# Retention loop: scores, sums and state products two tiles behind the transposes instead of one, with three buffers for v

## The reference

```python
x = x + retention(layernorm(x))            # B, T, C = 4, 1024, 256; 16 heads of 16
q, k, v = split(h @ w_qkv.T)               # h is the normed x
q, k = rope_xpos(q, k)                     # a rotation with a decay, per head
scores = einsum('bhtd,bhsd->bhts', q, k) * 16 ** -0.5
scores = scores * decay_mask               # causal, gamma ** (t - s) per head
y = einsum('bhts,bhsd->bhtd', scores, v)
yn = group_norm(y)                         # over a head's 16 channels and all T
out = (silu(h @ w_gated.T) * yn) @ w_proj.T
```

## Time and profile before

| | us |
|---|---|
| median of 3 runs | 1362.44 (1359.52 to 1365.13) |
| span of the profiled execution | 1357.2 |
| TensorE busy, share of the span | 1148.5, 85% |
| VectorE busy | 926.0, 68% |
| ScalarE busy | 613.3, 45% |
| GpSimd busy | 551.3, 41% |

### The profile page before, as it was taken

The page is one execution under the profiler, slowest core; times in us unless marked ns, Lnnn a source line. Parts: engine busy times, 40 slices in busy tenths (PEclk is TensorE's granted clock), DMA queues, the critical chain, the costliest instruction groups (busy, mean ns, idle before and its releaser), DMA issues. The chain is left out here.

```text
span 1357.2 us, 34954 instructions
## 1 busy us (share of the span) xinstructions
PE 1148.5 (85%) x14041; PEld 820.0 (60%) x14041; DVE 926.0 (68%) x1959; ACT 613.3 (45%) x1310; POOL 551.3 (41%) x537
## 2 busy tenths in 40 slices
PE   7999999976599999478999898898996658999970
PEld 4677777754488888235555555555554437888860
DVE  4778787757765656568678695968756376565646
ACT  2334343313255555144737455474635233555544
POOL 3333333202377776324151432415141115777750
PEclk9999999978699999698999999999999778999995
DMA  8032222108743332200000001000000095333338
GB/s 302 24 126 93 81 90 83 64 1 296 248 169 104 103 105 90 75 31 3 33 3 33 24 12 33 3 33 4 1 3 2 18 389 166 103 104 101 104 101 345
DMA packets 50683, 125.66 MB, mean 93 GB/s; under 512 B 7649, under 2 KB 26977, under 8 KB 47713
## 3 DMA queue, kind: packets, MB, share of 16 engines
q1 hardware_dynamic: 36896, 86.20, 17.7%
q0 software_dynamic: 13632, 37.24, 8.7%
HBM read 79.63 MB, written 43.78 MB: 91 GB/s over the span
## 5 line engine op out<-in xcount | busy, mean ns | idle before, releaser
L1090 POOL DMA_INDIRECT ffn_xs<-xn_rows,ffn_from_row x142 | 137.6, 969 | 123.7 <-DVE ffn_second_y_at L1472 81.0
L1098 POOL DMA_INDIRECT y_rows<-ffn_ys,ffn_to_row x142 | 140.1, 987 | 55.1 <-issue 35.4
L1253 PE MATMUL ffn_ps_h<-ffn_w_high,ffn_xst 128*128 x568 | 155.3, 396 | 0.6 <-issue 0.6
L1500 DVE TENSOR_TENSOR ffn_act_in<-ffn_silu_g,ffn_ps_h 128x256 f32<-128x256 f32 x142 | 59.9, 422 | 139.0 <-ACT ffn_silu_g L1132 139.0
L1132 ACT ACTIVATE ffn_silu_g<-ffn_ps_h 128x256 f32<-128x256 f32 x142 | 54.8, 386 | 144.3 <-PE ffn_ps_h L1253 144.3
L1273 PE MATMUL ffn_ps_o<-ffn_w,ffn_act_t 128*128 x284 | 117.2, 435 | 0.5 <-DVE ffn_act_t L1505 0.5
L1253 PEld LDWEIGHTS ffn_ps_h<-ffn_w_high,ffn_xst 128*128 128x128 f32 x568 | 97.4, 190 | 18.2 <-issue 1.1
L1833 POOL TENSOR_TENSOR rec_mixed_w<-rec_mixed_w,rec_xnt 128x512 f32<-128x512 f32 x16 | 17.2, 1091 | 207.5 <-DVE rec_mixed_w L2634 207.5
L1253 PE MATMUL ffn_ps_h<-ffn_w_low,ffn_xst 128*128 x284 | 89.8, 398 | 0.0
L644 DVE TENSOR_TENSOR ret_probs<-ret_score,ret_causal 128x2048 f32<-128x2048 f32 x32 | 73.3, 2292 | 18.7 <-PE ret_score L485 18.7
L1275 PE MATMUL ffn_ps_o<-ffn_w,ffn_act_t 128*128 x284 | 79.2, 279 | 0.0
(11 more groups left out here) (353 smaller groups left out, 2894.8 us busy)
## 6 DMA issues: line engine op xcount, KB each, us to landing
home<-y_rows SPq DMA_DIRECT2D x30, 512.0 KB, 5.0
w_split<-home SPq DMA_DIRECT2D x24, 512.0 KB, 4.1
ffn_w_high<-w_split SPq DMA_DIRECT2D x8, 1024.0 KB, 8.8
ffn_w_low<-w_split SPq DMA_DIRECT2D x8, 1024.0 KB, 10.7
ffn_w<-w_split SPq DMA_DIRECT2D x8, 1024.0 KB, 14.4
home<-in_f_w SPq DMA_DIRECT2D x12, 512.0 KB, 6.1
xn_rows<-home SPq DMA_DIRECT2D x12, 512.0 KB, 11.7
out<-x SPq DMA_DIRECT2D x8, 512.0 KB, 5.7
```

What stands on the lines that cost most here:

```text
L1090: pool.indirect_dma_start(xs[:, n % SLOTS, :], None, xn_rows[:], bass.IndirectOffsetOnAxis(ap=from_row[:, n:n + 1], axis=0)) \
L1098: pool.indirect_dma_start(y_rows[:], bass.IndirectOffsetOnAxis(ap=to_row[:, m:m + 1], axis=0), ys[:, m % SLOTS, :], None).then_inc(ys_stor ...
L1253: mm = pe.matmul(ps_h[:, u % 2, :], one_pass(xst[:, u % 2, part, k, :]), one_pass(w1[w_part][k][:, bass.ds(e, E_COLUMNS)]), start=(part + ...
L1500: dve.tensor_tensor(act_in[:, u % 2, :], silu_g[:, u % 2, :], ps_h[:, u % 2, FF:2 * FF], ALU.mult) \
```

## The change

TensorE's list for tile i becomes: transposes of x of i, scores of i-2, gate of i, the group norm's variance or the output's matmul, the projection of q and k of i, transposes of q and k of i-1, the projection of v of i, the group mean (t = 2) or the fourth output matmul (t = 7), outputs of i-2. The loop has two turns more at the end. `outputs` makes state times q for both halves, then the state product, then all sums. The state product moves to the bank of y, and a function `sums_read` makes its user wait for the y copy and for `add_state` of the tile before. `roped`, `v` and `v_heads` get three buffers. The gate is made before v, and its copy ahead of v's. VectorE does mask before rotate, and spread_q a tile later; group-norm steps move (`gn_half` of the second half to t = 2, `gated` to t = 4 and 5, the moments of the next batch to the end of t = 6). In GpSimd's list sum_state is a tile later and stands ahead of ln_root.

```diff
-        roped = sb("roped", [P, 2, 2 * C])
+        roped = sb("roped", [P, BUFFERS, 2 * C])
         rope_t1 = sb("rope_t1", [P, 2 * C])
         rope_t2 = sb("rope_t2", [P, 2 * C])
-        v = sb("v", [P, 2, C])
-        v_heads = sb("v_heads", [P, 2, NH, PAIR])
+        v = sb("v", [P, BUFFERS, C])
+        v_heads = sb("v_heads", [P, BUFFERS, NH, PAIR])
...
-        ps_state = ps_qkt[:, 0:KT * PAIR]
         ps_yp = ps("ps_yp", [P, BANK])
-        ps_y = ps_yp[:, 0:C]
+        ps_y, ps_state = ps_yp[:, 0:C], ps_yp[:, C:C + KT * PAIR]
...
                     pool.wait_ge(rope_parts, (i + 1) * 3)
-                    if i >= 2:
-
-                        pool.wait_ge(y_in_psum, i - 1)
-                    pool.tensor_tensor(roped[:, i % 2, :], rope_t1[:], rope_t2[:], ALU.add).then_inc(rope_done, 1)
+                    if i >= BUFFERS:
+
+                        pool.wait_ge(y_in_psum, i - BUFFERS + 1)
+                    pool.tensor_tensor(roped[:, i % BUFFERS, :], rope_t1[:], rope_t2[:], ALU.add).then_inc(rope_done, 1)
...
                 ln_root_first()
                 ln_root(0)
-                for i in range(TILES):
+                for i in range(TILES + 2):
                     b, t = step_of(i)
+                    if state_of(i - 3):
+                        sum_state(i - 3)
+                    if i >= TILES:
+                        continue
                     if t == TPB - 2 and b < B - 1:
                         ln_root(b + 1)
-                    if state_of(i - 2):
-                        sum_state(i - 2)
                     sum_rotation(i)
...
-                    if i >= 2:
-                        y_out(i - 2)
-                    v_out(i)
+                    gate_out(i)
                     if b > 0 and t == 4:
                         normed(b - 1, 0)
-                    gate_out(i)
-                    qk_out(i)
+                    if i >= 1:
+                        qk_out(i - 1)
+                    v_out(i)
                     if b > 0 and t == 4:
                         normed(b - 1, 1)
                     if 5 <= i < 5 + 2 * PIECES and i % 2 == 1:
                         split_high((i - 5) // 2)
+                    if i >= 2:
+                        y_out(i - 2)
+                qk_out(TILES - 1)
                 y_out(TILES - 2)
...
+                def sums_read(i):
+
+                    if i >= 1:
+                        pe.wait_ge(yt_ready, i)
+                        if states_before(i):
+                            pe.wait_ge(state_masked, states_before(i))
+
                 def outputs(i):
                     b, t = step_of(i)
                     pe.wait_ge(v_ready, (i + 1) * 3)
+                    sums_read(i)
+                    n_pairs = pairs_through(i + 2)
+                    if n_pairs:
+                        pe.wait_ge(x_added, n_pairs)
+                    n_steps = gn_read_through(i + 2)
+                    if n_steps:
+                        pe.wait_ge(gn_step, n_steps)
+                    if t >= 2:
+                        pe.wait_ge(state_ready, sums_before(i))
+                    for k in range(KT if t >= 1 else 0):
+                        for g in range(GROUPS):
+                            rows = slice(g * PAIR, (g + 1) * PAIR)
+                            pe.matmul(ps_y[rows, k * P:(k + 1) * P], state[rows, k, :], qkt[rows, i % 2, k, :],
+                                      start=(k == 0), stop=False, skip_group_check=True)
                     if t < TPB - 1:
-
-                        pe.wait_ge(qkt_ready, min(i + 2, TILES))
                         for k in range(KT):
                             for g in range(GROUPS):
                                 rows = slice(g * PAIR, (g + 1) * PAIR)
                                 own = slice(k * P + g * PAIR, k * P + (g + 1) * PAIR)
                                 mm = pe.matmul(ps_state[rows, k * PAIR:(k + 1) * PAIR],
-                                               roped[:, i % 2, C + own.start:C + own.stop], v[:, i % 2, own],
-                                               start=True, stop=True)
+                                               roped[:, i % BUFFERS, C + own.start:C + own.stop], v[:, i % BUFFERS, own],
+                                               start=(t == 0 and k == 0), stop=True, skip_group_check=True)
                         mm.then_inc(state_in_psum, 1)
-                    if i >= 1:
-                        pe.wait_ge(yt_ready, i)
-
-                        n_pairs = pairs_before(i + 2)
-                        if n_pairs:
-                            pe.wait_ge(x_added, n_pairs)
-                        n_steps = gn_read_before(i + 2)
-                        if n_steps:
-                            pe.wait_ge(gn_step, n_steps)
-                    if t >= 1:
-                        pe.wait_ge(state_masked, states_before(i))
-                    if t >= 2:
-                        pe.wait_ge(state_ready, sums_before(i))
+                    pe.wait_ge(probs_ready, i + 1)
                     for k in range(KT):
-                        for g in range(GROUPS if t >= 1 else 0):
-                            rows = slice(g * PAIR, (g + 1) * PAIR)
-                            pe.matmul(ps_y[rows, k * P:(k + 1) * P], state[rows, k, :], qkt[rows, i % 2, k, :],
-                                      start=True, stop=False)
-                        if k == 0:
-                            pe.wait_ge(probs_ready, i + 1)
                         for h in range(2):
                             for g in range(GROUPS):
                                 mm = pe.matmul(ps_y[g * PAIR:(g + 1) * PAIR, k * P:(k + 1) * P],
-                                               v_heads[:, i % 2, k * HPT + 2 * g + h, :], probs[:, g, k, h, :],
-                                               start=(h == 0 and t == 0), stop=(h == 1))
+                                               v_heads[:, i % BUFFERS, k * HPT + 2 * g + h, :], probs[:, g, k, h, :],
+                                               start=False, stop=(h == 1), skip_group_check=True)
                     mm.then_inc(y_in_psum, 1)
...
-                for i in range(TILES):
+                for i in range(TILES + 2):
                     b, t = step_of(i)
-                    transpose_x(i)
+                    if i < TILES:
+                        transpose_x(i)
+                    if i >= 2:
+                        scores(i - 2)
+                    if i == 0:
+                        project_qk(i)
+                        pe.wait_ge(early_consts_loaded, 16 * len(early_consts))
+                    if i < TILES:
+                        gate(i)
+                    if i == TPB - 1:
+                        pe.wait_ge(consts_loaded, 16 * len(consts))
+                    if 0 < b < B and t in (3, 5, 6, 7):
+                        sums_read(i - 2)
+                        if t == 3:
+                            group_variance(b - 1)
+                        else:
+                            projection(b - 1, t - 5, ps_yp)
+                    if 0 < i < TILES:
+                        project_qk(i)
+                    if 1 <= i <= TILES:
+                        transpose_qk(i - 1)
+                    if i < TILES:
+                        project_v(i)
+                    if 0 < b < B and t == 2:
+                        sums_read(i - 2)
+                        group_mean(b - 1)
+                    if 0 < b < B and t == TPB - 1:
+                        pe.wait_ge(x_added, b * PAIRS - 1)
+                        projection(b - 1, PAIRS - 1, ps_yp)
                     if i >= 2:
                         outputs(i - 2)
-                    project(i)
-                    if i == TPB - 1:
-                        pe.wait_ge(consts_loaded, 16 * len(consts))
-                    if b > 0 and t in (2, 3, 5, 6, 7):
-
-                        pe.wait_ge(yt_ready, i - 1)
-                    if b > 0 and t == 2:
-                        group_mean(b - 1)
-                    if b > 0 and t == 3:
-                        group_variance(b - 1)
-                    if b > 0 and t >= 5:
-                        projection(b - 1, t - 5, ps_yp)
-                    if i >= 1:
-                        scores(i - 1)
-                    gate(i)
-                    if b > 0 and t == TPB - 1:
-                        pe.wait_ge(x_added, b * PAIRS - 1)
-                        projection(b - 1, PAIRS - 1, ps_yp)
-                    transpose_qk(i)
-                outputs(TILES - 2)
-                scores(TILES - 1)
-                outputs(TILES - 1)
                 pe.wait_ge(yt_ready, TILES)
...
                     dve.wait_ge(state_in_psum, states_before(i + 1))
-                    if t == 0:
-
-                        if i > 0:
-                            dve.wait_ge(y_in_psum, i)
-                    elif t >= 2:
+
+                    dve.wait_ge(yt_ready, i + 1)
+                    if t >= 2:
...
```

(38 more changed lines are left out.)

79 lines of the change are left out of this document (24 added, 55 removed).

## The result

The changed kernel takes **1381.0 us** (median of 4 runs, 1379.65 to 1384.59) against 1361.95 of the kernel before (4 runs beside it): ratio **1.0142**, 95% interval 1.0112 to 1.0173. That is slower by over 0.5%, and above the forecast's 1363 and its range of 1351 to 1373. Both were run once more, with two of the experiments, and gave the same picture: 1380.76 against 1360.44, ratio 1.0152 (1.0095 to 1.0208).

The account below looks back on a forecast made before the run. TensorE's queue was taken as the bound. Batch 0 -5.2, batches 1 to 3 +2.15, +1.85, +0.7, end +1.1 sum to +0.6 on 1357.2: 1357.8, median 1363 us; own range 1357 to 1369, with part of the rivals 1351 to 1373.

Parts of the forecast that it names:

- The side of the gain: Plain tile of retention on TensorE: 7.99 - 0.44 - 0.13 - 0.29 - 0.07 = 7.06 us.
- The copy's wait: TensorE ahead of the state products: waiting for ScalarE's copy of transposed q and k gets covered, -0.44 us per plain tile.
- The forms: Fewer changes of matmul array form in TensorE's state products and sums: 1.82 for 2.11 us, -0.29 per plain tile.
- Rival 3: TensorE's sums: the forms save nothing, a plain tile is 7.35 us, +7 over 24 tiles, 1370; chance 0.10.
- Batch 0: Tiles 2 to 7 of the first batch: 42.2 us against 47.4, -5.2.
- The port: VectorE instructions with two SBUF inputs stand still under GpSimd's; scores wait 3.1 us in t3, 1.4 more in t4.
- Rival 1: GpSimd and VectorE instructions fall between each other, the port costs little: -9 to -12 us, 1352; chance 0.26.
- Rival 2: GpSimd starts ahead of spread_q, which loses the port: 3.5 us a batch, +10.5, 1373; chance 0.16.
- Step 1: Third buffer and the bank shared by y and the state product: claimed to cost nothing by themselves.
- Step 2: Tile 7 of batch 0: moved ln_root and split on GpSimd make sum_state late, +0.4 us.
- Step 3: VectorE beside GpSimd: rotation sum and split fall under spread_q, x_low, gn_variance and gated; holds for two SBUF inputs.
- Step 4: TensorE's granted clock: 1.00, the upper level of 2.4 GHz; waits of 3.1 us in t3, 1.4 in t4.

Follow-up runs that it names:

- halves apart: Against the kernel with all five edits: state and head parts of a tile's sums alternate by half again, as in the kernel before; 1348.54 us, ratio 0.9950 to before.
- moving the split: Against the changed kernel: GpSimd starts each weight-split piece ahead of the rotation's sum, beside VectorE's masking and rotation; 1360.83 us, ratio 1.0009 to before.
- bank undone: Against the changed kernel: the state product goes back into the bank of the q/k transposes, with its waits of before; 1371.36 us, ratio 1.0087 to before.
- moments earlier: Against the changed kernel: VectorE makes the next batch's norm moments in tile 6 ahead of its masking, not at its end; 1374.36 us, ratio 1.0107 to before.
- wait filled: Against the changed kernel: 24 unit-matrix transposes on TensorE ahead of the third tile's scores in every batch after the first; 1368.39 us, ratio 1.0054 to before.
- all five edits: Changed kernel with moments earlier, bank undone, split moved, q spread earlier and group norm's power moved on GpSimd; 1342.65 us, then with complete sums 1339.40, ratio 0.9868 to before.
- second traces: Both kernels traced once more without any edit; retention ends at 325.8 us in the changed kernel and 308.0 in before; changed again 1380.76 us, ratio 1.0152.

## Why the prediction was wrong, point by point

**The side of the gain was right, and undersized.** The plain tile is 6.77 for the forecast 7.06. The copy's wait and the gate copy's wait went as said (no idle time in the plain tile). The forms gave 0.40 by the run with the halves apart, where the sum had 0.29: the 0.11 of the state product's own changes was missed. The other 0.17 of the miss lie ahead of the sums, in the gate, the q/k transposes and the projections. Rival 3 (the forms save nothing) is out. Batch 0 came out at -5.05 for -5.2 (-3.55 by the first traces), and that is luck: the plain tiles gained more than forecast, and the last tile lost 2 to 4 us, where the forecast had +0.4.

**The port was right in mechanism and place.** t2, t3 and t4 as forecast were 8.12, 10.46, 8.47; without the clock's fall they are 8.52, 10.12, 8.37. The scores' wait is 3.07 for 3.1, the wait in t4 is 1.50 for 1.4, t6 is 9.51 for 9.35. Rival 1 (the port costs little) was tested by moving the split: with it there, retention takes 18 us more, the falls of the clock included. Rival 2 is out: where the spreading of q and the rotation's sum meet, it is the sum that pays (1538 ns on the page's mean for 1.27).

**Step 1 that failed: "The third buffer and the bank that y and the state product now share cost nothing by themselves."** The bank put a wait for the state's masking ahead of the group matmuls and of each projection, and that masking is queued on VectorE behind the gated halves, the statistics and the norm. Price: 1.0 us in each of t5 and t6; 6.0 us of retention by the bank undone. A second term was missing in t5, and it is not the bank's. The forecast has the gated pair held "until 30.6", which is 3.6 us into t5 on its own count (t5 starts at 27.05), and in the trace it is 3.66. The projection that reads the pair stands behind the gate, some 2.5 us into the tile, and the sum for t5 has no wait for it. With the bank undone that wait is there by itself, 1.21 us. Both together are the 2.27 us of the row at 112.23, and t5 is 10.99 for 9.67.

**Step 2: "+0.4 in tile 7, where GpSimd's moved ln_root (...) and split make sum_state late", in batch 0 alone.** The moments went behind the rotation, to the end of t6, and the next user of their root is the norm at the head of t7. The forecast followed the queue of GpSimd (the state's sum) and not the one who waits for the root. For t7 of batches 1 and 2 it gave 11.50, and they take 13.78; with the moments earlier they take 11.38. Price by that run: 5.6 us of retention, and 6.9 us over the three last tiles.

**Step 3: holds were looked for in instructions with two inputs in SBUF alone.** The norm has one, with two columns as scalars, and it took 1.34 and 2.42 us beside GpSimd for 0.40. No run separates the price of this hold from that of the late root. I had quoted half a rule: the Trainium skill, GPSIMD Engine Reference, "Key points", names contention with VectorE instructions with two SBUF inputs and also with those in a 2-port performance mode, which fits a norm that is held; that it ran in that mode no row shows.

**Step 4, the largest: the clock was taken as 1.00 throughout.** It was so in every window of before, where TensorE's longest idle time between tiles 2 and 31 was 0.56 us. I put a wait of 3.1 us into t3 and another into t4 and priced them by their own length. With the wait filled, and nothing else changed, retention ends 11.1 us earlier: of the 17.8 lost, some 11 are work done at 1.2 GHz behind waits. The forecast's own waits should have raised the question. The prices of the four steps overlap, as the run with all five edits shows, and do not add up to the 17.8.

**Ends.** Start: forecast 0, -0.9 by the second traces. End: +1.1, measured +1.8. Behind retention: forecast 0, 2 to 3 us in the medians.

In sum by the second traces, forecast and measured: batch 0 -5.2 and -5.05, batch 1 +2.15 and +7.65, batch 2 +1.85 and +9.36, batch 3 +0.7 and +4.99, ends +1.1 and +0.85: +0.6 and +17.8. None of the rivals had the shared bank, the late root or the clock in it, so the range could not hold the time.
